# Attention scores formed a second time in turned form, in place of turning the exponentials, in a float32 attention and mixture-of-experts kernel

## The reference, cut to what matters

```python
q, k, v = (split_heads(x @ W + b) for W, b in ((Wq, bq), (Wk, bk), (Wv, bv)))    # 4 x 512 tokens, 16 heads of 32
attn = einsum('bhqd,bhkd->bhqk', q, k) / sqrt(32)
attn = attn - slopes[:, None, None] * (511 - arange(512))                        # ALiBi
attn = where(causal, attn, finfo.min)
out = einsum('bhqk,bhkd->bhqd', softmax(attn), v) @ Wo + bo
x = layernorm(x + out)
logits = x @ Wr + br                      # 4 experts, the best one per token is used
y = (silu(x @ Wg[e]) * (x @ Wu[e])) @ Wd[e] * softmax(logits)[e]                 # 512 -> 2048 -> 512
x = layernorm(x + y)
```

## Time and profile before

| | us |
|---|---|
| median of three runs | 1240.27 |
| the profiled execution | 1241.71 |
| its span, first to last instruction | 1239.9 |
| attention loop, 30.5 to 473 | 442.5 |
| last rows, router, lists, 473 to 518 | 45.0 |
| experts, 518 to the end | 721.9 |

### The profile page before, as it was taken

The page is one execution under the profiler, slowest core; times in us unless marked ns, Lnnn a source line. Parts: engine busy times, 40 slices in busy tenths (PEclk is TensorE's granted clock), DMA queues, the critical chain, the costliest instruction groups (busy, mean ns, idle before and its releaser), DMA issues.

```text
span 1239.9 us, 27812 instructions
## 1 busy us (share of the span) xinstructions
PE 1157.9 (93%) x8682; PEld 1054.7 (85%) x8682; DVE 765.3 (62%) x1974; ACT 571.7 (46%) x1411; POOL 308.1 (25%) x451
## 2 busy tenths in 40 slices
PE   5998999999999986599999999999999999999994
PEld 4888888888898875598899889989988988998893
DVE  3676778677767775566654664665466366546664
ACT  3677766676767674252332323233233233323353
POOL 5400211201020123532321330331133033113336
PEclk9999999999999997699999999999999999999997
DMA  8222233222323231443132222313212221321202
GB/s 271 69 52 68 68 75 116 53 54 77 95 61 77 68 105 42 128 128 101 47 93 71 60 78 69 93 54 93 71 54 84 70 83 55 87 85 52 86 36 101
DMA packets 109684, 100.10 MB, mean 81 GB/s; under 512 B 12847, under 2 KB 81839, under 8 KB 109552
## 3 DMA queue, kind: packets, MB, share of 16 engines
q1 hardware_dynamic: 104784, 87.85, 25.5%
q0 software_dynamic: 3040, 9.18, 2.2%
q10 hardware_dynamic: 1728, 1.31, 0.3%
HBM read 64.74 MB, written 9.18 MB: 60 GB/s over the span
## 4 chain that ended last, share of the span: by engine, by line
PE 71%; POOL 7%; DMA 5%; ACT 5%; issue 5%; DVE 4%; SPq 3%; ACTq 0%; DVEq 0%; POOLq 0%
PE bank L814 36%; PE bank L596 13%; PE bank L839 7%; POOL up_lo L1501 6%; PE bank L734 4%; PE bank L717 4%; DMA up_raw<-in_Wu_dram 3%; PE bank L826 3%; PE bank L706 2%; SPq L488 2%; ACT probs L922 1%; DMA q_stack<-qk_lo 1%; DVE probs L1181 1%; ACT up_hi L954 1%; PE bank L743 1%
## 5 line engine op out<-in xcount | busy, mean ns | idle before, releaser
L814 PE MATMUL bank<-up_hi,xsT_hi 128*128 x1216 | 356.0, 293 | 9.2 <-POOL up_lo L1501 8.5
L814 PE MATMUL bank<-up_hi,xsT_lo 128*128 x1216 | 344.4, 283 | 0.0
L814 PE MATMUL bank<-up_lo,xsT_hi 128*128 x1216 | 344.3, 283 | 0.0
L1501 POOL TENSOR_TENSOR up_lo<-up_raw,up_hi 128x256 fp32r<-128x256 f32 x241 | 170.9, 745 | 483.1 <-ACT up_hi L954 482.9
L1333 DVE SCALAR_TENSOR_TENSOR h_tok<-bank,row_weight,silu 128x128 f32<-128x128 f32 x304 | 93.4, 347 | 295.0 <-ACT silu L1033 292.6
L814 PEld LDWEIGHTS bank<-up_hi,xsT_hi 128*128 128x128 f32 x1216 | 233.0, 192 | 15.9 <-issue 15.7
L814 PEld LDWEIGHTS bank<-up_hi,xsT_lo 128*128 128x128 f32 x1216 | 233.8, 192 | 0.3
L814 PEld LDWEIGHTS bank<-up_lo,xsT_hi 128*128 128x128 f32 x1216 | 233.3, 192 | 0.0
L1033 ACT ACTIVATE silu<-bank 128x256 f32<-128x256 f32 (+1 forms) x160 | 59.6, 372 | 364.4 <-PE bank L814 364.4
L1350 DVE TENSOR_TENSOR y<-bank,y 128x512 f32<-128x512 f32 x295 | 199.0, 690 | 0.5
L922 ACT ACTIVATE probs<-probs,neg_max 128x512 f32<-128x512 f32 (+3 forms) x256 | 136.5, 558 | 59.8 <-DVE neg_max L1181 58.7
(11 more groups left out here) (176 smaller groups left out, 2070.3 us busy)
## 6 DMA issues: line engine op xcount, KB each, us to landing
up_raw<-in_Wg_dram SPq DMA_DIRECT2D x64, 256.0 KB, 3.7
up_raw<-in_Wu_dram SPq DMA_DIRECT2D x64, 256.0 KB, 4.5
down_raw<-in_Wd_dram SPq DMA_DIRECT2D x64, 256.0 KB
k_stack<-qk_hi SPq DMA_DIRECT2D x128, 64.0 KB, 2.0
q_stack<-qk_hi SPq DMA_DIRECT2D x128, 64.0 KB, 2.0
k_stack<-qk_lo SPq DMA_DIRECT2D x64, 64.0 KB, 2.0
q_stack<-qk_lo SPq DMA_DIRECT2D x64, 64.0 KB, 2.0
x_tok<-in_x_dram SPq DMA_DIRECT2D x3, 1024.0 KB, 6.4
```

The lines of the kernel that those rows point to most:

```text
L814: mm = pe.matmul(bank[:, n * 2 * P:(n + 1) * 2 * P], a[:, s, k, :], up_w[w][k][:, :, :].rearrange("p a f -> p (a f)")[:, bass.ds(at, 2 * P ...
L1501: pool.tensor_tensor(up_w[1][k][:, e, :], up_raw[:, idx % NUPS, k, :, :].rearrange("p g f -> p (g f)"), up_w[0][k][:, e, :].bitcast(F32), ...
```

## The change: what it does

The exponentials are no longer turned. Instead the scores are made twice. The first product is the old one, with queries as rows. Only the row maxima are kept from it, in `neg_max`. PE turns the four maxima columns of a head into four rows (`row_of_maxima`), ACT scales them (`copy_row`), and SP writes them with a small DMA as a 97th row of `q_stack` (`load_row`). `k_stack` has ones in its 97th row. The second product (`unit_turned`) takes `k_stack` as weights and `q_stack` as columns, so its result has keys as rows and queries as columns, already with the maximum taken off. The units of that second pass are key tiles: tile 2 (256 columns), tile 0 (512), tiles 1 and 3 (384 and 128). DVE adds the causal mask to the diagonal blocks (`unit_masked`), ACT takes the exponential from PSUM (`unit_exp`) and copies the high part (`unit_split`), and POOL now makes the low part (`unit_low`). The values product has one high and one low product per key tile, with up to 512 columns, nine per head in place of 20.

The lags grow: the second pass comes 7 steps after the first (`LAG`), the values 10 steps after it (`VL`), and the loop has 202 steps. There are six stack slots in place of four. The row of maxima is handled in every third step (4, 7, 10, ... ), and in those same steps, behind it, SP loads up to two stacks. A stack is due there once K and Q of its group were taken and the slot's old head is through its second pass. The planner now spreads K and Q so that they end by step 9 of the group (`KQ_DUE`).

```diff
--- before.py
+++ after.py
...
-UNIT_TILES = ((3,), (0, 1), (2,))
-UNITS = [(g, h, tiles) for g in range(NG) for h in range(GH) for tiles in UNIT_TILES]
-U = len(UNITS)
-PER_HEAD = len(UNIT_TILES)
+QUERY_TILES = ((3,), (0, 1), (2,))
+KEY_TILES = ((2,), (0,), (1, 3))
+PER_HEAD = len(QUERY_TILES)
+U = NB * NH * PER_HEAD
 PER_GROUP = GH * PER_HEAD
 T0 = NT - QT
 LAST = NB - 1
 DONE = (GPB - 1) * GH
 AHEAD = 6
 NUPS, NDS, NX = 2, 4, 3
-VLAG, NP = 4, 3
-UP_STEPS = (1, 3)
+LAG, VL = 7, 10
+STEPS, WORK = U + VL, U + LAG
+ROW_AT = LAG - PER_HEAD
+NP, NSTK, NMAX = 4, 6, 3
+CENTRE = 192
+UP_STEPS = (5, 9)
...
+def key_spans(tiles):
+    at = 0
+    for j in tiles:
+        yield j, at, SEQ - j * P
+        at += SEQ - j * P
...
+KQ_STEP, KQ_DUE = 2, 9
...
+        later_kq = 2 * 12 * 213 if step < KQ_STEP and g else 0
+        last = max([n for n, j in enumerate(queue) if j[0] in ("K", "Q")], default=-1)
+        due = later_kq + sum(sum(cost_of(j)) for j in list(queue)[:last + 1])
+        if due or left and now_job[0] in ("K", "Q"):
+            due += sum(c for _, c in left)
+        return max((owed() + later_kq) / (2 * (PER_GROUP - step) - half), due / (2 * max(KQ_DUE - step, 1) - half))
...
-        k_stack = p1.put("k_stack", [3 * HD, GH, SEQ], F32R)
-        q_stack = p1.put("q_stack", [3 * HD, GH, SEQ], F32R)
+        stacks_at = p1.at
+        k_stack = p1.put("k_stack", [3 * HD + 1, NSTK, SEQ], F32R)
+        q_stack = p1.put("q_stack", [3 * HD + 1, NSTK, SEQ], F32R)
...
+            def load_stacks(hd):
+                g = hd // GH
                 sp.wait_ge(s_side_dve, max(done("K", g), done("Q", g)))
-                sp.wait_ge(s_scores, scores_count(g - 1, h))
+                if hd >= NSTK:
+                    sp.wait_ge(s_sT, (hd - NSTK + 1) * PER_HEAD)
                 for n in (WK, WQ):
-                    load_part(h, n, False)
-                    load_part(h, n, True)
+                    load_part(hd, n, False)
+                    load_part(hd, n, True)
+            def load_row(hd):
+                sp.wait_ge(s_maxrow, hd + 1)
+                sp.dma_start(q_stack[3 * HD:3 * HD + 1, hd % NSTK, :].rearrange("p (i n) -> p i n", i=QT).bitcast(F32),
+                             max_row[:, hd % 2, :].bitcast(F32)).then_inc(s_rowin[hd % 2], 16)
...
-            stacks = deque((g, h) for g in range(1, NG) for h in range(GH))
-            x_due = 2
-            for u in range(U + VLAG):
-                if x_due <= NB and plan.flushed.get(("OP", (x_due - 2) * QT + QT - 1), U + 9) <= u:
-                    sp.wait_ge(s_side_dve, done("OP", (x_due - 2) * QT + QT - 1))
-                    if x_due < NB:
-                        load_x(x_due)
-                    else:
+            next_stack = GH
+            for u in range(STEPS):
+                if is_head_step(u, ROW_AT):
+                    load_row((u - ROW_AT) // PER_HEAD)
+                    for _ in range(2):
+                        if (next_stack < NB * NH and plan.flushed[("Q", next_stack // GH)] <= u
+                                and (next_stack < NSTK or (next_stack - NSTK) * PER_HEAD + PER_HEAD - 1 + LAG < u)):
+                            load_stacks(next_stack)
+                            next_stack += 1
...
-                while stacks:
-                    g, h = stacks[0]
-                    if plan.flushed[("Q", g)] > u or scores_count(g - 1, h) > u + 1:
-                        break
-                    stacks.popleft()
-                    load_stacks(g, h)
...
+            def unit_turned(u):
+                hd, n = divmod(u, PER_HEAD)
+                slot, bank = hd % NSTK, banks[2 + u % 2]
+                if n == 0:
+                    pe.wait_ge(s_rowin[hd % 2], 16 * (hd // 2 + 1))
+                if u == 0:
+                    pe.wait_ge(s_onesrow, 1)
+                if u >= 2:
+                    pe.wait_ge(s_exp, u - 1)
+                for j, at, width in key_spans(KEY_TILES[n]):
+                    mm = pe.matmul(bank[:, at:at + width], k_stack[:, slot, j * P:(j + 1) * P], q_stack[:, slot, j * P:SEQ],
                                    start=True, stop=True)
-                mm.then_inc(s_scores, 1)
-            def unit_transpose(u):
-                blocks = sum(i + 1 for i in UNITS[u][2])
-                bank = banks[2 + u % 2]
-                pe.wait_ge(s_exp, u + 1)
-                if u >= 2:
-                    pe.wait_ge(s_pTlo, u - 1)
-                for j in range(blocks):
-                    mm = pe.transpose(bank[:, j * P:(j + 1) * P], probs[:, u % NP, j * P:(j + 1) * P], ident[:, :])
-                mm.then_inc(s_pT, 1)
...
+            def row_of_maxima(hd):
+                pe.wait_ge(s_biased, (hd + 1) * PER_HEAD)
+                pe.transpose(banks[2 + (hd + 1) % 2][0:QT, 2 * P:3 * P], neg_max[:, hd % NMAX, :], ident[:, :]).then_inc(s_maxT, 1)
...
-                for i, at, _ in spans(tiles):
-                    for j in range(i + 1):
-                        for part in (pT_hi, pT_lo):
-                            mm = pe.matmul(bank[0:VW, i * P:(i + 1) * P], v[:, g // 2 % 2, j, g % 2 * GH + h, :],
-                                           part[:, u % NP, at + j * P:at + (j + 1) * P],
-                                           start=(j == 0 and part is pT_hi), stop=(j == i and part is pT_lo))
+                opens, closes = KEY_TILES[0][0], KEY_TILES[-1][-1]
+                for j, at, _ in key_spans(KEY_TILES[n]):
+                    for part in (pT_hi, pT_lo):
+                        for c0, c1 in ((0, opens * P), (opens * P, SEQ)) if j == 0 and part is pT_hi else ((j * P, SEQ),):
+                            mm = pe.matmul(bank[0:VW, c0:c1], v[:, g // 2 % 2, j, g % 2 * GH + h, :],
+                                           part[:, u % NP, at + c0 - j * P:at + c1 - j * P],
+                                           start=(j == opens and part is pT_hi), stop=(j == closes and part is pT_lo))
...
+            def copy_row(hd):
+                act.wait_ge(s_maxT, hd + 1)
+                if hd == 0:
+                    act.wait_ge(s_keyset, 1)
+                else:
+                    act.wait_ge(s_masked, (hd - 1) * PER_HEAD + 1)
+                if hd >= 2:
+                    act.wait_ge(s_rowin[hd % 2], 16 * (hd // 2))
+                act.activation(max_row[:, hd % 2, :], banks[2 + (hd + 1) % 2][0:QT, 2 * P:3 * P], ACT.Identity,
+                               scale=1.0 / SLOPE[hd % NH], bias=row_shift[0:QT, 0:1]).then_inc(s_maxrow, 1)
...
-                act.wait_ge(s_biased, u + 1)
-                for i, at, width in spans(tiles):
-                    ex = act.activation(probs[:, u % NP, at:at + width], probs[:, u % NP, at:at + width], ACT.Exp, scale=-1.0,
-                                        bias=neg_max[:, u % NP, i:i + 1])
-                ex.then_inc(s_exp, 1)
-            def unit_transposed(u):
-                blocks = sum(i + 1 for i in UNITS[u][2])
-                act.wait_ge(s_pT, u + 1)
+                hd, n = divmod(u, PER_HEAD)
+                act.wait_ge(s_masked, u + 1)
                 if u >= NP:
                     act.wait_ge(s_pv, u - NP + 1)
-                act.activation(pT_hi[:, u % NP, 0:blocks * P], banks[2 + u % 2][:, 0:blocks * P], ACT.Copy).then_inc(s_pThi, 1)
+                else:
+                    act.wait_ge(s_counting, 1)
+                for j, at, width in key_spans(KEY_TILES[n]):
+                    ex = act.activation(probs[:, u % NP, at:at + width], banks[2 + u % 2][:, at:at + width],
+                                        ACT.Exp, scale=SLOPE[hd % NH], bias=key_bias[:, hd % NH, j:j + 1])
+                ex.then_inc(s_exp, 1)
+            def unit_split(u):
+                n = sum(width for _, _, width in key_spans(KEY_TILES[u % PER_HEAD]))
+                act.wait_ge(s_exp, u + 1)
+                act.activation(pT_hi[:, u % NP, 0:n], probs[:, u % NP, 0:n], ACT.Copy).then_inc(s_pThi, 1)
...
+            def unit_masked(u):
+                hd, n = divmod(u, PER_HEAD)
+                dve.wait_ge(s_sT, u + 1)
+                if n == 0 and hd + 1 < NB * NH:
+                    dve.wait_ge(s_maxT, hd + 2)
+                if u == 0:
+                    dve.wait_ge(s_keyset, 2)
+                starts = [at // P for _, at, _ in key_spans(KEY_TILES[n])]
+                blocks = banks[2 + u % 2][:, :].rearrange("p (b n) -> p b n", n=P)[:, 0:starts[-1] + 1:starts[-1] or 1, :]
+                dve.tensor_tensor(blocks, blocks, causal[:, :].unsqueeze(1).to_broadcast([P, len(starts), P]),
+                                  ALU.add).then_inc(s_masked, 1)
...
+            def unit_low(u):
+                n = sum(width for _, _, width in key_spans(KEY_TILES[u % PER_HEAD]))
+                pool.wait_ge(s_pThi, u + 1)
+                pool.tensor_tensor(pT_lo[:, u % NP, 0:n], probs[:, u % NP, 0:n],
+                                   pT_hi[:, u % NP, 0:n].bitcast(F32), ALU.subtract).then_inc(s_pTlo, 1)
```

(16 more changed lines are left out.)

376 lines of the change are left out of this document (207 added, 169 removed).

## The result

The changed kernel takes 1335.92 us, the median of four runs (1331.04 to 1340.35), against 1240.09 for the kernel before beside it (four runs, 1237.31 to 1243.05). The ratio is 1.0771, with a 95% interval of 1.072 to 1.0823. It is slower by 96 us. The forecast was 1264 with a range of 1222 to 1292: the direction was right, the size about a quarter of what came.

What follows compares the result with a forecast made beforehand. PE was taken to set the pace of the attention loop, 422.8 of 442.5 us. The terms -32 + 49 + 10 - 15 + 8 + 4 gave +24 us, hence 1264 us, range 1222 to 1292.

Steps and rivals of the forecast that it cites:

- PE's work: Attention loop: fewer turns and value products outweigh the added turned scores, -32 us (-24 to -38) for 64 heads.
- The stop at the boundary: Between groups, PE stops for late stacks behind the row of maxima: 14 times 3.5 us, +49 us (35 to 57).
- Two waits behind it: SP's stack issues delay the next row; ACT's next K waits for the fourth stack: +10 us (0 to 24).
- What the stops swallow: PE's old 19.7 us of visible waits lie largely at the same group boundaries and vanish: -15 us (-20 to 0).
- The three idle terms: PE's idle time in the loop: boundary stop +49, two waits behind it +10, swallowed old waits -15 us.
- PE's clock: Stops at group boundaries may each lose some 1.6 us to half clock, most short ones don't: +8 us (0 to 22).
- Filling and draining: Loop's ends: ten steps of turned scores and values left instead of four, with ACT-set steps: +4 us (-6 to +10).
- The other engines: Loop busy times: DVE 264 us, ACT about 330, POOL 283, all well under 400 and hidden by the lag.
- A: Boundary stop stays at its floor and swallows old waits and the two behind it: -19, 1221 us, chance 22%.
- B: Late boundary stop, waits behind it whole, clock falling at each boundary: +60, 1300 us, chance 15%.
- C: POOL sets the loop's pace, its 512-column subtraction slowing beside DVE: +70, 1310 us, chance 5%.
- D: The change's gains and losses cancel: 1234 to 1246 us, chance 8%.

Runs made afterwards that it cites:

- experiment 4: Changed kernel with K and Q due in step 7, not 9: 1285.86 us; or with SP loading one stack in any due step: 1273.49 us.
- experiment 9: Changed kernel, lags 6 and 9: with ACT issuing the row 1266.16 us; helpful edits combined 1298.97; combined without the rule barring a stack ahead of a row 1266.13.
- Experiments 1 to 3: 1: kernel before, stacks begun late, 1378.39 us; 2: changed kernel, 14 unused products at 13 boundaries, 1326.05; 3: late stacks plus those products, 1375.26.
- experiment 6: Changed kernel, one stack in any step, K and Q due in 8: no stack ahead of a row, 1269.5 us; or row issued by ACT, 1283.15 us.
- experiment 7: Changed kernel, one stack in any step, due in 8, x ahead of stacks on SP, values' sum ahead of bias and mask on DVE: 1306.29 us.
- experiment 8: Changed kernel, one stack in any step, due in 8, low part of each head's 256-column unit on DVE in place of POOL: 1269.77 us.
- experiments 5 and 7: 5: changed kernel, one stack in any step, K and Q due in 8, 1273.79 us, or in 7, 1288.26; 7: two orders turned, 1306.29.
- experiment 1: Kernel before, with SP beginning the next group's stacks only after PE's last score product of the group: 1378.39 us, ratio 1.1087.

## Why the prediction was wrong in size, by its steps

- **PE's work**, -32 (-24 to -38): right. The account gives -31, and all versions with the second pass and without added products lie between 389 and 400 of work.
- **The stop at the boundary**, +49 (35 to 57): right in place, number and mechanism, 14 waits released by the DMA of q_stack, and small: 59.3 us, just over its range, 4.2 each for 3.5. Step 10's chain took 7.5 us for 6.7 in the one shown. Removing it brought 62 us back with its clock (experiment 4), and returning 37 us of it cost 33 (experiment 9).
- **Two waits behind it**, +10: turned scores waited for the row 2.5 us. The other is ACT's, and there it is large:

```profile
ACT probs L1027 <- DVE bank L1300: 144.3, 89, 5.8
ACT qk_hi L983 <- DMA q_stack<-qk_lo: 19.9, 7, 6.9
```

  In the kernel before, the second of these waits was:

```profile
ACT qk_hi L897 <- DMA q_stack<-qk_lo: 14.3, 9, 2.8
```

  ACT held K seven times for a stack, up to 6.9 us, with exponentials behind it, where the longest before was 2.8. What that cost PE isn't shown. Of the 144 us of the first line, in which ACT waits for the mask, 70 lie at PE's 16 long stops.
- **What the stops swallow**, -15: wrong in sign. Waits for the sum of the values rose from 6 to 13.6 us, and others came. I had taken the old waits as lying at the boundaries, but of the 18 us of idle time in the old loop only one pause of 1.2 us is the wait for a stack, and 4.0 lie in the last group, behind all boundaries. That the new ones come from a longer pipeline, which has more places that stand a step apart, is my reading. The three idle terms came to +44 and measured +80.
- **PE's clock**, +8 (0 to 22): this step failed most. Measured +50. I priced a stop's clock by one pause of 2.1 us at 1.6 us, and by taking 8 of the 22 us I let nearly two thirds of the stops be free of it, because the old loop had a mean clock of 1.00. But its waits were short. All 16 long stops of the changed kernel have a half-clock stretch behind them, 39 us in all or 2.4 each, and the other 13 us stand behind shorter pauses and in the last group, for which the prediction had no term. Experiments 1 to 3 show that long stops bring the clock down with the second pass and without it. They don't show that the second pass is without effect: with it, versions whose longest pause is 2.0 and 2.7 us lose 39 and 48 us (experiments 6 and 7), and no version without it was run with as many short pauses. The rule that the prediction cited from the Trainium skill (TensorE: Matmul & The Clock Gate, "HAM oscillation") would have made the term 22 with my price for a stop; the trace agrees with it for these long stops, 16 of 16, and it was the better guide than my mean.
- **Filling and draining**, +4: too small. From the last group's first scores to the last value product the loop takes 50.5 us for 32.4. These three lines are the kernel before, the changed one, and that of one stack in any step:

```profile
438.50:470.90 32.40, 28.43 (x248) 24.68 (x246) 22.10 (x69) 22.63 (x57) 7.58 (x13) 1.00 0.23 65
```

```profile
517.10:567.60 50.50, 44.67 (x229) 36.74 (x229) 24.66 (x87) 33.78 (x79) 30.03 (x37) 0.78 0.27 76
```

```profile
446.10:497.00 50.90, 43.01 (x232) 34.42 (x230) 26.98 (x93) 35.10 (x83) 32.44 (x41) 0.83 0.26 72
```

  Of the 18 us some 5.5 are work put off by the lag and 11 are clock (8 in the third). These 18 us are a place and are within the account's three parts, not beside them. The best versions without the boundary's stop still lose 24 to 32 us, and in the one read here the end is the larger part of it: with one stack in any step, the 15 groups ahead of the last take 417.4 us where they took 408.0, and the end costs the rest.
- **The other engines**: ACT 326 for 330, POOL 283 for 283, DVE 281 for 264. DVE's miss of 17 us is in two forms above all. The masks take 42.2 + 29.7 = 72 us where the forecast had 64 x 0.92 = 59. And its read of the accumulator takes 142 ns where the kernel before has 83, now that the biased scores go back to the bank, 256 x 0.059 = 15 us:

```profile
L1181 DVE DVE_READ_ACCUMULATOR2_ANT neg_max<- 128x1 f32 x256 | 21.3, 83 | 0.0
```

  These are sums of durations, which overlap on DVE, so they come to more than the 17 us of busy time.
- **Rivals.** A fell: the mean stop of 4.2 is over its 3.1. B was the nearest, with the late stop and the clock at every boundary, and still gave 1300: it, too, had the low price of a stop's clock and the swallowed waits. C fell with POOL's durations and in experiment 8, D with the result.

What stays open: why pauses of the same sum cost 23 us of clock in one version and 39 in another (52 us of idle time, experiment 6), or 30 and 48 (60 us, experiments 5 and 7), and what makes up the last 30 us of idle time, which moved from row to values to exponentials as each was eased. No version without the row of maxima was run, so its full price isn't known.

## What to carry to other kernels

A stop of PE has two prices, its length and the half-clock stretch behind it: read the clock in the stretches behind long stops, and don't take it from a loop's mean in which stops are short. Then sum it over the whole loop too, since many short pauses lost as much here (48 us with none over 2.7). When an order is changed, count back from each consumer to the last step at which a queue may still start its transfer; one step of SP's rule was worth 33 us here. The work saved on PE was kept for the most part, 21 to 31 us of the 32 forecast, but the longer pipeline paid for it in its drain and in new waits.

## What was not expected of the hardware

- Adding 46 us of products that nothing uses made the changed kernel 10 us faster, because the clock's loss fell from 52 to 26 us.
- Behind stops of 2.8 to 7 us the granted clock was 0.50 for some 3 to 7 us each time, in the changed kernel and in experiment 1; pauses of 2.0 and 2.5 us in the version of one stack in any step were followed by a clock of 1.00.
- With no pause over 2.7 us, the loop of experiment 7 lost 48 us to the clock, and with none over 2.0 the one with ACT's issue lost 39.
- A DMA issued by ACT took 581 ns of its queue, about what SP takes, and counts in no busy time.
- DVE's read of its accumulator took 142 ns in the changed kernel, where the biased scores are written back to their bank, and 83 ns before, where they are written to `probs`.
